# Second attention with three score banks each way, an earlier shift, and loads begun before the stage seams

## What is computed

```python
xn = layernorm(x)
x = x + gated_delta(xn) + local_layers(xn)      # gated delta rule, 6 heads; then 6 layers of window-32 attention and GELU feed-forward
xn = layernorm(x)
x = x + windowed_attention(xn) + column_mixture(xn)
# the end of gated_delta
o = o * silu(gate)
o = o * rsqrt(mean(o * o) + 1e-5) * norm_weight
return o @ o_w.T
# windowed_attention: 16 heads of 8 values, each token looks 128 tokens back and 128 ahead
attn = softmax((q @ k_win) / sqrt(8));  out = (attn @ v_win) @ Wo + bo
```

## Time and profile before

| | us |
|---|---|
| median of 3 runs | 2992.68 (2975.16 to 2995.49) |
| the profiled execution | 2996.28 |
| its span, first to last instruction | 2994.5 |
| PE busy | 2617.1 (87%) |
| POOL busy | 1833.5 (61%) |
| DVE busy | 1735.6 (58%) |
| ACT busy | 1473.3 (49%) |

### The profile page before, as it was taken

One profiled execution on the slowest core, in us unless ns is written; L12 is line 12 of the kernel. 1 busy time (PEld: TensorE's weight loads), 2 busy tenths in 40 slices (PEclk: granted clock), 3 DMA queues, 4 the chain that ended last, 5 costly groups with the idle time before them and its releaser, 6 DMA issues. The chain is left out here.

```text
span 2994.5 us, 97379 instructions
## 1 busy us (share of the span) xinstructions
PE 2617.1 (87%) x40447; PEld 1766.4 (59%) x40447; DVE 1735.6 (58%) x3395; ACT 1473.3 (49%) x2703; POOL 1833.5 (61%) x3112
## 2 busy tenths in 40 slices
PE   4868999975889999999999999999999997699977
PEld 1227888973566666666666666666666664345445
DVE  5831232212767777777777777777777773555524
ACT  3722222211556666666666666666666664134432
POOL 0035676601888888888887888888888882122211
PEclk9967898755999999999999999999999999769868
DMA  1001111102111122221212122212211110000000
GB/s 32 0 22 36 37 38 36 37 23 103 43 45 47 53 58 69 53 59 45 70 53 59 45 69 54 60 46 71 55 47 45 43 45 23 14 3 4 3 13 15
DMA packets 113168, 124.97 MB, mean 42 GB/s; under 512 B 40783, under 2 KB 71263, under 8 KB 111967
## 3 DMA queue, kind: packets, MB, share of 16 engines
q1 hardware_dynamic: 111808, 117.52, 14.3%
q10 hardware_dynamic: 926, 1.27, 0.1%
HBM read 35.89 MB, written 8.91 MB: 15 GB/s over the span
## 5 line engine op out<-in xcount | busy, mean ns | idle before, releaser
L1719 POOL TENSOR_TENSOR l_rot_a<-l_rot_a,l_rot_b 128x512 f32<-128x512 f32 x384 | 483.9, 1276 | 112.2 <-DVE l_rot_b L1579 111.8
L1207 PE MATMUL l_A<-l_wts,l_H 128*128 128x512 f32 x768 | 413.9, 623 | 25.8 <-ACT l_H L1520 21.3
L1573 DVE TENSOR_TENSOR l_rot_a<-l_A,l_tab 128x512 f32<-128x512 f32 x384 | 264.9, 690 | 292.0 <-ACT l_sq L1439 279.7
L1728 POOL TENSOR_TENSOR l_qk<-l_rot_a,l_rn 128x512 f32<-128x512 f32 x384 | 388.7, 1044 | 21.2 <-POOLq L1766 21.2
L1439 ACT ACTIVATE l_sq<-l_A 128x512 f32<-128x512 f32 x384 | 230.9, 601 | 131.1 <-PE l_A L1207 127.0
L1445 ACT ACTIVATE l_pT<-l_T 128x512 f32<-128x512 f32 x192 | 108.8, 595 | 374.2 <-PE l_T L1253 373.8
L1579 DVE TENSOR_TENSOR l_rot_b<-l_A,l_tab 128x512 f32<-128x512 f32 x384 | 261.3, 681 | 0.0
L1583 DVE TENSOR_REDUCE l_ss<-l_sq 128x8 f32<-128x512 f32 x384 | 259.4, 676 | 0.0
L1308 PE MATMUL l_T<-ident,l_qk 128*128 128x128 f32 x1536 | 212.1, 281 | 22.2 <-POOL l_qk L1728 16.7
L1308 PEld LDWEIGHTS l_T<-ident,l_qk 128*128 128x128 f32 x1536 | 176.9, 144 | 86.9 <-issue 58.5
L1791 POOL TENSOR_TENSOR l_pn<-l_sd,l_rs 128x1024 f32<-128x1024 f32 x96 | 182.9, 1905 | 69.1 <-DVE l_rs L1601 69.0
(11 more groups left out here) (340 smaller groups left out, 5743.5 us busy)
## 6 DMA issues: line engine op xcount, KB each, us to landing
l_vw<-l_vn SPq DMA_DIRECT2D x384, 128.0 KB
l_vw<-l_vn SPq DMA_DIRECT2D x360, 64.0 KB
l_wts<-in_l_wts SPq DMA_DIRECT2D x18, 650.0 KB, 5.1
c_lower_out<-c_amt SPq DMA_DIRECT2D x16, 384.0 KB, 2.5
c_inv<-c_first_in SPq DMA_DIRECT2D x16, 384.0 KB, 3.3
l_tab<-in_l_tables SPq DMA_DIRECT2D x6, 1024.0 KB, 5.2
l_wts<-in_l_wts SPq DMA_DIRECT2D x6, 635.5 KB, 5.2
result<-x SPq DMA_DIRECT2D x4, 256.0 KB, 2.3
```

Of the source, the lines that this page charges most:

```text
L1207: pe.matmul(A[j % 2][:], cols(m), w_of(m)[:, C_QKV + 512 * j:C_QKV + 512 * j + 512], start=True, stop=True).then_inc(pq_done, 1)
L1573: dve.tensor_tensor(rot_a[p][:, j, :].rearrange("p (a d) -> p a d", d=DH), src.rearrange("p (a d) -> p a d", d=DH), table[:, a, t:t + 1, : ...
L1719: pool.tensor_tensor(rot_a[m % 2][:, j, :], rot_a[m % 2][:, j, :], rot_b[:, j, :], ALU.add).then_inc(rot_rdy, 1)
L1728: pool.tensor_tensor(qk[:, j, :].rearrange("p (a d) -> p a d", d=DH), rot_a[p][:, j, :].rearrange("p (a d) -> p a d", d=DH), rn[p][:, 8 * ...
```

## The change

1. The clearing of `xnT`'s edge and `vT` moves from DVE, behind the load of x, to POOL, beside that load, and one barrier goes.
2. `normalise`: the roots are computed on DVE, and centring and scaling become one instruction for each tile (16) in place of 4 + 4.
3. The weights of `delta_inputs`, `windowed_attention` and `column_mixture` are loaded one stage earlier: in the first and second `normalise`, and in the attention. Their semaphores and buffers belong to an outer scope, which adds two clears with a barrier each.
4. `delta_outputs`: the norm weight is multiplied into `wo` (POOL), and the root is applied after the product; `gate` itself is turned, two tiles at a time, two pairs ahead of the product. DVE squares and sums, and does one multiply-add for each tile.
5. `local_layers`: all of layer 0's weights are loaded ahead of its tables, and ACT's first copies no longer wait for weights.
6. `windowed_attention`: `s_ps` goes from 4 banks to 3 and `t_ps` from 2 to 3, both used in turn by n = 16 s + h; `shift` stands behind two maxima in place of four; the fourth `scores` of a step moves behind `turn_maxima`.

```diff
-def normalise(nc, x, xn, xnT, ident, tag):
+def normalise(nc, x, xn, xnT, ident, tag, begin_loads):
...
+        @block.sync
+        def _(sp):
+            begin_loads(sp)
...
+            rsqrt(dve, rstd[:], mv[:, :, 1], tmp[:], 0.0, 1e-5, rs_rdy, 0, tick)
             dve.wait_ge(rs_rdy, RSQRT_STEPS)
+            for t in range(NT):
+                dve.tensor_scalar(xn[:, t, :], x[:, t, :], mv[:, t, 0:1], rstd[:, t:t + 1], ALU.subtract, ALU.mult).then_inc(xn_rdy, 1)
...
+                @block.gpsimd
+                def _(pool):
+                    pool.memset(xnT[:, :, 0:KCONV - 1], 0.0)
+                    pool.memset(vT[:], 0.0).then_inc(cleared, 1)
+                    pool.wait_ge(cleared, 1)
...
+            sp.dma_start(wo[:], dram["d_wo"]).then_inc(w_ld, 16)
+            for c, (c0, cn) in enumerate(VB):
+                sp.dma_start(nw[0:cn, c:c + 1], dram["d_nw"][:, c0:c0 + cn].rearrange("o d -> d o")).then_inc(w_ld, 16)
+            sp.dma_start(x[:], dram["x"].rearrange("(t p) d -> p t d", p=P)).then_inc(x_ld, 16)
...
+            for t in range(NT):
+                dve.wait_ge(y_done, QUAD * (t // QUAD) + QUAD)
+                dve.scalar_tensor_tensor(x[:, t, :], yp[t // QUAD][:, t % QUAD, :], rstd[:, t:t + 1], x[:, t, :], ALU.mult, ALU.add)\
+                   .then_inc(x_rdy, 1)
...
+            for c, (c0, cn) in enumerate(VB):
+                pool.tensor_scalar(wo[0:cn, c, :], wo[0:cn, c, :], nw[0:cn, c:c + 1], None, ALU.mult).then_inc(wo_rdy, 1)
+            pool.wait_ge(ms_rdy, NT)
+            rsqrt(pool, rstd[:], ms[:], tmp[:], 0.0, 1e-5, rs_rdy, 0, tick)
...
+            turn(0)
+            turn(1)
+            pe.wait_ge(wo_rdy, len(VB))
+            for u in range(NT // PAIR):
+                if u + 2 < NT // PAIR:
+                    turn(u + 2)
+                project(u)
...
-            weights(0, 0)
+            for part in range(4):
+                weights(0, part)
             tables(0)
-            weights(0, 1)
             sp.dma_start(maskb[:], dram["l_mask"]).then_inc(const_ld, 16)
-            for part in (2, 3):
-                weights(0, part)
             tables(1)
...
-            act.wait_ge(w_ld[0], w_need(0))
-            act.wait_ge(w_ld[1], w_need(1))
...
-        AHEAD = 2
+        AHEAD, BANKS = 2, 3
...
-                if n >= GROUP:
-                    pe.wait_ge(mx_rdy, n - GROUP + 1)
+                if n >= BANKS:
+                    pe.wait_ge(mx_rdy, n - BANKS + 1)
...
-                if n >= 2:
-                    pe.wait_ge(p_rdy, n - 1)
+                if n >= BANKS:
+                    pe.wait_ge(p_rdy, n - BANKS + 1)
...
-                    for h in range(GROUP):
+                    for h in range(BANKS):
                         scores(s, h)
                 if has(s - 1):
                     turn_maxima(s - 1)
+                if has(s):
+                    scores(s, BANKS)
...
-                if has(s):
-                    for h in range(GROUP):
-                        maxima(s, h)
-                if has(s - 1):
-                    shift(s - 1)
-                for h in range(GROUP, AH):
+                for h in range(AH):
+                    if h == AHEAD and has(s - 1):
+                        shift(s - 1)
                     if has(s):
                         maxima(s, h)
...
-            pe.wait_ge(first_ld, 16 * len(first))
+            pe.wait_ge(loaded, LOADED)
```

More of the change, by code:

```diff
@@ L8 @@
 from contextlib import ExitStack
+from dataclasses import dataclass
 import numpy as np
@@ L1900, in windowed_attention, with load_weights @@
         TURNED, VALUED = 2, 4
-        AHEAD = 2
+        AHEAD, BANKS = 2, 3
         STEPS = NT + VALUED
+        def load_weights(sp):
+            for dst, name in loads:
+                sp.dma_start(dst, dram[name]).then_inc(w_ld, 16)
+            sp.dma_start(row_b[:].rearrange("p a d -> p (a d)"), dram["a_row_b"].broadcast_to([P, 2 * D])).then_inc(w_ld, 16)
+        normalise(nc, x, xn, lambda t, n: xnT[:, P * t:P * (t + n)], ident, "n1", load_weights)
+        s_ps = [ps(f"a_s{i}", [P, 512]) for i in range(BANKS)]
+        t_ps = [ps(f"a_t{i}", [P, 512]) for i in range(BANKS)]
+        proj_ps = (s_ps[0], s_ps[1], s_ps[2], t_ps[2])
+        m_ps = ps("a_m", [P, 512])
+        o_ps = ps("a_o", [P, 512])
         block = ctx.enter_context(nc.Block())
@@ L1923, in _ @@
         def _(sp):
[L1924 to L1926 removed]
+            load_mixture(sp)
         @block.tensor
@@ L2190, with mixture_weights, load, column_mixture @@
 STRIP = P // CB
-def column_mixture(nc, x, xn, xnT, ident, dram):
+@dataclass
+class Mixture:
+    w: object
+    pw: object
+    gw1: object
+    gw2: object
+    bcol: object
+    rows: object
+    emb: object
+    spread: object
+    order: object
+    loaded: object
+    load: object
+def mixture_weights(nc, ctx, dram):
+    sb, ps, sem = buffers(nc, ctx)
+    w = sb("m_w", [P, CB * P])
+    pw = sb("m_pw", [P, CB, D])
+    gw1 = sb("m_gw1", [P, GATE_H])
+    gw2 = sb("m_gw2", [GATE_H + 1, NCOL])
+    bcol = sb("m_bcol", [P, CB + 1])
+    rows = sb("m_rows", [P, 3, D])
+    emb = sb("m_emb", [NCOL, D])
+    spread = sb("m_spread", [P, P])
+    order = sb("m_order", [P, NCOL])
+    loaded = sem("m_loaded")
+    def load(sp):
+        for dst, name in ((gw1[:], "m_gw1"), (w[:], "m_w"), (bcol[:], "m_bcol"), (emb[:], "m_emb"), (gw2[:], "m_gw2"),
+                          (pw[:], "m_pw"), (spread[:], "m_spread")):
+            sp.dma_start(dst, dram[name]).then_inc(loaded, 16)
+        sp.dma_start(order[:], dram["m_order"].broadcast_to([P, NCOL])).then_inc(loaded, 16)
+        sp.dma_start(rows[:].rearrange("p a d -> p (a d)"), dram["m_rows"].broadcast_to([P, 3 * D])).then_inc(loaded, 16)
+    return Mixture(w, pw, gw1, gw2, bcol, rows, emb, spread, order, loaded, load)
+def column_mixture(nc, x, xn, xnT, ident, dram, mixture):
     with ExitStack() as ctx:
         sb, ps, sem = buffers(nc, ctx)
-        w = sb("m_w", [P, CB * P])
-        pw = sb("m_pw", [P, CB, D])
-        gw1 = sb("m_gw1", [P, GATE_H])
-        gw2 = sb("m_gw2", [GATE_H + 1, NCOL])
-        bcol = sb("m_bcol", [P, CB + 1])
-        rows = sb("m_rows", [P, 3, D])
-        emb = sb("m_emb", [NCOL, D])
-        spread = sb("m_spread", [P, P])
-        order = sb("m_order", [P, NCOL])
+        w, pw, gw1, gw2, bcol = mixture.w, mixture.pw, mixture.gw1, mixture.gw2, mixture.bcol
+        rows, emb, spread, order, loaded = mixture.rows, mixture.emb, mixture.spread, mixture.order, mixture.loaded
+        LOADED = 16 * 9
         embT = sb("m_embT", [P, NCOL])
@@ L2248, in _ @@
         def _(sp):
-            for dst, name in first:
-                sp.dma_start(dst, dram[name]).then_inc(first_ld, 16)
-            for dst, name in late:
-                sp.dma_start(dst, dram[name]).then_inc(late_ld, 16)
             for g in range(NG):
@@ L2322, in _ @@
         def _(act):
-            for dst, name in gates:
-                act.dma_start(dst, dram[name]).then_inc(gate_ld, 16)
-            act.dma_start(order[:], dram["m_order"].broadcast_to([P, NCOL])).then_inc(gate_ld, 16)
-            act.dma_start(rows[:].rearrange("p a d -> p (a d)"), dram["m_rows"].broadcast_to([P, 3 * D])).then_inc(gate_ld, 16)
-            act.wait_ge(first_ld, 16 * len(first))
+            act.wait_ge(loaded, LOADED)
             def column(n):
@@ L2510, in program @@
             xnT = second.enter_context(nc.sbuf_tensor("xnT2", [P, NT * P], F32))
-            normalise(nc, x, xn, lambda t, n: xnT[:, P * t:P * (t + n)], ident, "n1")
-            windowed_attention(nc, x, xnT, ident, dram)
-            column_mixture(nc, x, xn, xnT, ident, dram)
+            mixture = mixture_weights(nc, second, dram)
+            windowed_attention(nc, x, xn, xnT, ident, dram, mixture.load)
+            column_mixture(nc, x, xn, xnT, ident, dram, mixture)
 def kernel(L0_attn_hidden_states, L0_attn_q_w, L0_attn_k_w, L0_attn_v_w, L0_attn_a_w, L0_attn_b_w, L0_attn_g_w, L0_attn_o_w,
```

199 lines of the change are left out of this document (83 added, 116 removed).

## The result

The changed kernel takes 2886.48 us in the median of 4 runs (2868.53 to 2895.93), against 2994.09 us before (4 runs). The ratio is 0.9646, with a 95% interval of 0.9583 to 0.9708. The forecast was 2900, with a range of 2870 to 2936. The profiled executions have spans of 2885.9 and 2994.5 us, so 108.6 us less where the sum in the prediction said 92.7. The total is close, but the terms are not: the delta outputs were priced too high, the attention far too low, and the delta chunks and the mixture moved where the forecast had 0.

The account below looks back on a forecast made before the run. Stage by stage: waits at five seams, and in the attention two banks for the turned product, not an engine. Terms summed to -92.7 us, 2903.6 from the profiled 2996.3; against the median 2992.7 it said 2900, range 2870 to 2936.

Parts of the forecast that it names:

- Start, roots, loads: Start and normalises: clearing on POOL -4.9, roots on DVE -6.8 for both, earlier loads -6.3 and -5.7, clears +1.0 us.
- Local layers (-8): Head of the local layers: POOL free at 736.8, its four additions then run without pause; -8 us (-4 to -9).
- Delta outputs (-33): Delta outputs: PE runs without waits, 3 tiles at 2.0 us, 13 at 1.0 as the clock rises; -33 (-18 to -38).
- the clock stays at half: Rival, delta outputs: granted clock stays at half, -18 instead of -33, total 2915 us; chance 0.12.
- Attention: Windowed attention: three banks let DVE set the pace, about -2.0 us a full-clock step; sum -29 (-12 to -40).
- Shift and lone head cancel: 0: Attention step: earlier shift gains up to 1 us, the fourth scores standing alone costs as much; net 0.
- At half clock the gain of a step falls to about 1: Attention: a fifth of the steps run at half clock and gain less, adding +3.5 us to the sum.
- Mixture (0): Column mixture: PE starts 3.5 us earlier but waits for the embedding's operand, whose chain is not shorter; 0.
- PE's array as the bound: Rival, attention: PE's array is the bound, -12 instead of -29, total 2917 us; chance 0.16.
- Gains nothing: Rival, attention: PE's fixed order makes waits for a maximum hold up turned products, no gain, 2929 us; chance 0.05.
- Slower: Rival, attention: the new waiting pattern loses the full clock; about +22, total 3015 us; chance 0.02.
- More than forecast, 2883: Rival: denser attention keeps full clock and delta outputs take 0.7 us a tile, total 2883 us; chance 0.08.

## Why the prediction was right, and where its steps failed

*Start, roots, loads: right*, with -12.8 and -7.5 against -14.1 and -8.6. Only the roots were mis-sized: mostly 0.32 a step, 4.99 us in all, so -2.1 each instead of -3.4; and of the scalings, priced at "Nothing", PE's start shows 0.4.

*Local layers (-8): right*, at -7.4, by the mechanism named: POOL's tables and additions stand without a gap.

*Delta outputs (-33): direction right, size wrong.* The failed step is "Does the clock rise? ... so I let it rise here too". It did not; the stage is at 0.50 in 13 of 14 profiles, whether PE waits in it or not. This was one of the prediction's own signs of being wrong. The rival "the clock stays at half", held at 0.12, had -18, measured -21.3. The 0.99 that I leaned on in the earlier trace rows is of a stretch in which PE did nothing, right behind 3.83 us of turnings: it shows a rise there, but neither that it lasts nor that other work brings one, and the outputs' clock was already at half when they began. The prices per tile were good: 1.82 at half clock (2.0 predicted) and, in the one profile that had it, 1.03 at full (1.0).

*Attention (-29, measured -52.6, beyond the bound of -40): the pace was right, its parts were not, and the clock term had the wrong sign.* A full-clock step fell by 1.92 in the mean of five, with 2.0 forecast. The banks gave 1.6 to 2.1 of it (2.2 predicted). "Shift and lone head cancel: 0" failed: the lone head gave 0.3 in the mean without the shift and 0.4 to 0.6 with it, the shift about nothing. The step that failed is the clock: "At half clock the gain of a step falls to about 1 ...: +3.5" took the clock's shares over from before, and the stretch holds 0.90 in place of 0.79. Term by term, the first two steps cost 4.5 more than before (+3.5 predicted; +2.4 of it before the first shift). The next two, up to the shift of tile 3, gave 3.8 and 8.0 where 3 each were predicted; the second of them went from half clock to full. The twelve steps up to the shift of tile 15 fell by 37.8 us, with -24 + 3.5 predicted; at 1.92 each they would give 23, so about 15 is clock (an estimate from these rows). The rest up to the mixture gave 8.5, where 6 were predicted.

*Lone head and drain.* The 0.62 of the earlier trace rows stands in the changed kernel too, also where no other engine was waited for:

```profile
2671.17 0.69 PE L1955 MATMUL a_s<-a_kT,a_qT 32*32 32x288 f32 x8
...
2671.79 0.42 PE L1991 MATMUL a_o<-a_pT,a_v 128*32 128x128 f32 x8
```

The Trainium skill (TensorEngine Tiling (Array Packing), Key Properties) has TensorE drain at a change of tiling mode, and these rows agree with it. It was the smaller of two effects, since a wait for a maximum went away with it.

*Mixture (0): wrong by about +4.* "PE starts 3.5 us earlier and waits there: 0" held for the time of the turning: its operand is ready 13.2 us into the stage, before and after. But the sign given, "the mixture as long as before", did not come. It left out what comes behind the wait: the gate products took 7.01 us instead of 5.08, at half clock.

*Not in the prediction: the chunks' 11.1 us.* They lie within the scatter of that stage, whose code is unchanged, and no run shows them to be an effect of the change. Without them the profiles differ by 97.5, with the forecast's 92.7. That this is so close is in part luck: the 11.7 that the outputs lack and the 4.1 of the mixture were made up by 23.6 too much in the attention.

*The rivals.* PE's array as the bound, with -12: no, the step fell by 1.9. "Gains nothing": no. "Slower": not in this kernel, but the orders without the banks did lose the clock. "More than forecast, 2883" had the denser attention keeping full clock, which happened, together with outputs at 0.7 a tile, which did not.

## What to carry to other kernels

Count a bank ring as a round trip divided by its banks, and then look at what each engine has queued behind a new wait: here the third bank was worth 1.6 to 2.1 us a step, the place of one head 0.3 to 0.6, and a shift of DVE's order nothing that lasted. Compare the same step with the same step, at the same clock. Don't carry the clock of the profile before over to a part that gets denser or gets a new wait in front of PE: the attention rose from 0.79 to 0.90, and the mixture, with a wait of 3.33, fell from 0.78 to 0.73; nor count on a rise, as the outputs had none. Judge an edit by the length between marks in the stage it touches, and take the scatter of untouched stages as the error of the total.

## What the runs showed of the hardware that was not expected

- The granted clock of the attention, with the same instructions, went from 0.70 to 0.91 by their order and the banks alone, and the stretch from 328.4 to 237.0 us.
- Dense PE work does not always bring full clock: in the outputs PE ran 28 us without a gap at 0.50, and 52.8 us of work in 58.3 with twice as many products. The clock had fallen before the stage.
- A stage with unchanged code, PE busy nearly throughout, took 350 to 392 us from profile to profile, with a granted clock of 0.93 in the shortest and 0.82 where it took 389 to 392.
- Loads that come early can cost: in one profile a mixture whose PE started 7.3 us later was 3.6 us shorter, though the totals don't show it.
- A dependent small step on DVE takes 0.32 us with a tick counted between and 0.20 without.
